# Attention scores one head at a time on quarter row tiles of TensorE, with all key and query rows resident

## What is computed

```
q = ((seq2 + b_self) @ Wq + bq)                # per head: 128 queries x 8
k = (concat[seq1 + b_prev, seq2 + b_self] @ Wk + bk)
score_prev = q @ k[:l1].T * SCALE              # masked with -inf where key >= seq_len1
score_self = (q * k[l1:]).sum(-1) * SCALE
weights    = softmax(concat[score_prev, score_self])
attn       = weights[:-1] @ v[:l1] + weights[-1:] * v[l1:]
x          = x + attn @ Wo + bo
```

## Time and profile before

| | |
|---|---|
| runs | 465.1, 459.02, 459.02 us; median 459.02 |
| profiled execution | 456.68 us, span 454.9 us, mean granted clock of TensorE 0.967 |
| PE busy | 427.5 us (94%), 2280 products |
| DVE, ACT, POOL busy | 336.1, 279.9, 185.5 us |
| DMA | 30.70 MB, mean 67 GB/s |

### The profile page before, as it was taken

How to read it: one execution, slowest core, us unless ns; L and a number is a source line. 1 busy time by engine, 2 the same in 40 slices (tenths; PEclk the granted TensorE clock), 3 DMA queues, 4 the chain that set the end, 5 groups by cost and what they waited for, 6 DMA issues and landing times.

```text
span 454.9 us, 7748 instructions
## 1 busy us (share of the span) xinstructions
PE 427.5 (94%) x2280; PEld 326.0 (72%) x2280; DVE 336.1 (74%) x598; ACT 279.9 (62%) x563; POOL 185.5 (41%) x235
## 2 busy tenths in 40 slices
PE   7799799799999999999999999999999988798985
PEld 3688678578788888878888887788888554454553
DVE  4897577696787779777777887776787776576763
ACT  5777476766555666655565766555655676476672
POOL 0868667572232233322242224226477424333330
PEclk9989899899999999999999999999999998888898
DMA  5525224200002020000201000010222624666430
GB/s 166 162 75 159 89 74 141 67 26 1 1 20 74 2 70 1 22 0 0 89 3 53 16 0 1 1 46 33 62 72 59 153 75 142 171 160 162 116 108 25
DMA packets 27908, 30.70 MB, mean 67 GB/s; under 512 B 4293, under 2 KB 22313, under 8 KB 27881
## 3 DMA queue, kind: packets, MB, share of 16 engines
q1 hardware_dynamic: 26680, 29.99, 22.8%
q0 software_dynamic: 768, 0.28, 0.4%
q10 hardware_dynamic: 432, 0.10, 0.1%
HBM read 22.73 MB, written 7.35 MB: 66 GB/s over the span
## 4 chain that ended last, share of the span: by engine, by line
PE 75%; DMA 10%; DVE 5%; issue 3%; ACT 3%; POOL 2%; SPq 1%; DVEq 0%; ACTq 0%; POOLq 0%
PE acc_ps L526 7%; PE u_ps L526 6%; PE acc_ps L528 6%; PE acc_ps L527 6%; PE g_ps L526 6%; PE g_ps L528 6%; PE g_ps L527 6%; PE u_ps L528 6%; PE u_ps L527 6%; DMA w_raw<-in_L_cond_Wu 4%; DMA k_plain<-k_rows 3%; PE pv_ps L702 3%; PE st_ps L692 2%; DMA q_blocks<-max_rows 2%; PE s_ps L594 2%
## 5 line engine op out<-in xcount | busy, mean ns | idle before, releaser
L841 ACT ACTIVATE act_p<-g_ps 128x512 f32<-128x512 f32 x144 | 85.9, 597 | 112.5 <-PE g_ps L528 112.0
L1135 DVE TENSOR_TENSOR act_p<-act_p,u_ps 128x512 f32<-128x512 f32 x144 | 98.6, 685 | 72.0 <-PE u_ps L528 40.5
L1139 DVE TENSOR_TENSOR act_lo<-act_p,act_hi 128x512 fp32r<-128x512 f32 x144 | 121.7, 845 | 0.4 <-ACT act_hi L846 0.4
L1380 POOL TENSOR_TENSOR xg_lo<-xg,xg_hi 128x512 fp32r<-128x512 f32 x35 | 50.1, 1432 | 149.9 <-ACT xg_hi L851 149.9
L846 ACT ACTIVATE act_hi<-act_p 128x512 fp32r<-128x512 f32 x144 | 89.9, 624 | 7.2 <-DVE act_p L1135 6.9
L526 PE MATMUL u_ps<-xg_hi,w_split 128*128 128x512 f32 x144 | 56.8, 395 | 7.4 <-issue 7.4
L526 PE MATMUL acc_ps<-act_hi,w_split 128*128 128x512 f32 x144 | 59.0, 410 | 0.0
L526 PE MATMUL g_ps<-x_hi,w_split 128*128 128x512 f32 (+1 forms) x144 | 57.5, 399 | 0.6 <-DVE x_lo L1168 0.6
L528 PE MATMUL acc_ps<-act_hi,w_split 128*128 128x512 f32 x144 | 56.9, 395 | 0.0
L527 PE MATMUL acc_ps<-act_lo,w_split 128*128 128x512 f32 x144 | 56.7, 394 | 0.0
L527 PE MATMUL g_ps<-x_lo,w_split 128*128 128x512 f32 (+1 forms) x144 | 56.7, 394 | 0.0
(11 more groups left out here) (193 smaller groups left out, 683.1 us busy)
## 6 DMA issues: line engine op xcount, KB each, us to landing
k_blocks<-k_rows SPq DMA_DIRECT2D x32, 96.0 KB
q_plain<-q_rows SPq DMA_DIRECT2D x8, 384.0 KB
q_blocks<-q_rows SPq DMA_DIRECT2D x32, 96.0 KB
k_plain<-k_rows SPq DMA_DIRECT2D x8, 384.0 KB
w_raw<-in_L_cond_Wg SPq DMA_DIRECT2D x8, 256.0 KB, 2.7
w_raw<-in_L_cond_Wu SPq DMA_DIRECT2D x8, 256.0 KB, 2.6
w_raw<-in_L_cond_Wd SPq DMA_DIRECT2D x8, 256.0 KB, 2.9
q_rows<-rows_hi SPq DMA_DIRECT2D x16, 128.0 KB
```

The lines of the kernel that those rows point to most:

```text
L841: activation(act_p[k % ACTS][:], g_ps[k % 3][:], ACT.Silu).then_inc(silu_done, 1)
L1135: tt(act_p[k % ACTS][:], act_p[k % ACTS][:], u_ps[k % 3][:], ALU.mult).then_inc(prod_done, 1)
L1139: tt(act_lo[k % ACTS][:], act_p[k % ACTS][:], act_hi[k % ACTS][:].bitcast(F32), ALU.subtract).then_inc(act_lo_done, 1)
L1380: tt(xg_lo[e % 3][:], xg[:].rearrange("p b s -> p (b s)"), xg_hi[e % 3][:].bitcast(F32), ALU.subtract)\
```

## The change

- `k_blocks`, `q_blocks`, `k_plain`, `q_plain` go. One tile, `key_query`, holds keys and queries of all eight pairs: group i's 24 rows lie on partitions 32i to 32i + 23, each head j in its own columns. Row 24 is the mask (keys) or ones (queries), rows 25 and 26 are ones (keys) or the two parts of the maxima (queries). The mask thus comes with the product, and ACT's bias and POOL's `pick_mask` go.
- A score is a product of one head: 25 rows (27 in the transposed kind) x 128 weights x 128 columns, four for a group. `both_scores` issues a group of either kind in turns; the s kind works on another group (`GROUPS`), so on other partitions and in another bank. Where only one kind stands, the four come one after another.
- PE's order in a pass is new: both scores of groups 0 and 1, `turn_max`, `turn_attn`, weigh two groups, both scores of group 2, weigh two groups, both scores of group 3, `project`, `turn_pv`. The loop of PE is written out.
- SP loads pairs 0 to 5 during the last tile, as POOL's fills of `key_query` end (768 KB and nine DMAs a pair), and pairs 6 and 7 in passes 4 and 5. `place_max` moves from POOL's queue to SP's: two DMAs a batch instead of one. ACT copies the max rows after the first exponential instead of before it.

```diff
-            def scores(b, n, i, bank=None):
+            def rows(m, p, g, count, j, n):
+                return key_query[ROW_TILE * g:ROW_TILE * g + count, p, m, j, half(n)]
...
+            def score(n, p, i, j, bank=None):
+                return mm((s_ps[i % 2] if bank is None else bank)[:, j * S:(j + 1) * S],
+                          rows(1, p, GROUPS[i], MAX_ROW, j, n), rows(0, p, GROUPS[i], MAX_ROW, j, n), start=True, stop=True)
...
+            def score_t(n, p, i, j):
+                return mm(st_ps[i % 2][:, j * S:(j + 1) * S], rows(0, p, i, MAX_ROW + 2, j, n), rows(1, p, i, MAX_ROW + 2, j, n),
+                          start=True, stop=True)
...
+            def both_scores(b, n, p, i, s_next):
+                if not s_next:
+                    return scores_t(b, n, p, i)
+                wait_scores(b + 2, n + 2, i)
+                wait_scores_t(b, n, i)
+                for j in range(GJ):
+                    last = score(n + 2, p + 1, i, j)
+                    last_t = score_t(n, p, i, j)
+                last.then_inc(s_written, 1)
+                last_t.then_inc(st_written, 1)
...
-            def body(b, n, s_next=True, turn_next=True):
-                if s_next:
-                    for i in range(2):
-                        scores(b + 2, n + 2, i)
+            def body(b, n, p, s_next=True, turn_next=True):
+                both_scores(b, n, p, 0, s_next)
+                both_scores(b, n, p, 1, s_next)
                 if turn_next:
                     turn_max(b + 1, n + 1)
-                for i in range(2):
-                    scores_t(b, n, i)
                 last_tile_step(b, 1)
...
                 if n >= 2:
                     turn_attn(b - 2, n - 2)
-                if s_next:
-                    scores(b + 2, n + 2, 2)
-                    scores(b + 2, n + 2, 3)
-                scores_t(b, n, 2)
+                weigh(b - 1, n - 1, 0)
+                weigh(b - 1, n - 1, 1)
+                both_scores(b, n, p, 2, s_next)
...
# SP
+            def load_pair(p):
+                for m, src in enumerate((k_rows, q_rows)):
+                    for i in range(GI):
+                        sp.dma_start(key_query[ROW_TILE * i:ROW_TILE * i + ONES_ROW, p, m] ... , src[p, ...]).then_inc(pair_loaded[p % 2], 16)
+                sp.dma_start(key_query[ONES_ROW:128:ROW_TILE, p, 0] ... , mask_row[...]).then_inc(pair_loaded[p % 2], 16)
+            def place_max(b):
+                sp.wait_ge(max_copied, b + 1)
+                for c in range(2):
+                    sp.dma_start(key_query[MAX_ROW + c:128:ROW_TILE, b // 2, 1, :, b % 2 * S:(b % 2 + 1) * S].bitcast(F32),
+                                 max_rows[b % 2][c * H:(c + 1) * H]).then_inc(max_placed[b % 2], 16)
...
+            for b in range(B):
+                place_max(b)
+                if b == 2:
                     later_stores(NT - 1)
+                if b in (4, 5):
...
+                    load_pair(p)
+                if b % 2 and b >= 5:
+                    store_out(b - 5, b - 3)
```

More of the change, by code:

```diff
@@ L198, in build @@
         SMALLS = 2 * (GI * GJ + GI * GJ + GI * GJ + 2 * H + S + H) + 4 * H * (DH + 1)
[L200 to L211, removed]
+        key_query = sb2("key_query", [128, NP, 2, GJ, PAIR * S], F32R)
+        FILLS = [(p, -(-(SMALLS + (p + 1) * 2 * GJ * PAIR * S) // (2 * 3 * F))) for p in range(NP)]
         probs_t = [sb2(f"probs_t{n}", [128, GJ, S]) for n in range(4)]
@@ L269, in build @@
         blocks_filled = sem("blocks_filled")
[L270 to L271 removed]
+        pair_loaded = [sem(f"pair_loaded{n}") for n in range(2)]
         max_placed = [sem(f"max_placed{n}") for n in range(2)]
@@ L683, in _, with wait_scores_t, scores_t @@
                     turn_max(EARLY_TURN[k], EARLY_TURN[k])
[L686 removed]
+            def wait_scores_t(b, n, i):
                 if i == 0:
[L689 removed]
                     pe.wait_ge(max_placed[n % 2], placed(b, n))
                 wait(pe, exp_done, b * GI + i - 1)
[L692 to L693 removed]
+            def score_t(n, p, i, j):
+                return mm(st_ps[i % 2][:, j * S:(j + 1) * S], rows(0, p, i, MAX_ROW + 2, j, n), rows(1, p, i, MAX_ROW + 2, j, n),
+                          start=True, stop=True)
+            def scores_t(b, n, p, i):
+                wait_scores_t(b, n, i)
+                for j in range(GJ):
+                    last = score_t(n, p, i, j)
+                last.then_inc(st_written, 1)
+            def both_scores(b, n, p, i, s_next):
+                if not s_next:
+                    return scores_t(b, n, p, i)
+                wait_scores(b + 2, n + 2, i)
+                wait_scores_t(b, n, i)
+                for j in range(GJ):
+                    last = score(n + 2, p + 1, i, j)
+                    last_t = score_t(n, p, i, j)
+                last.then_inc(s_written, 1)
+                last_t.then_inc(st_written, 1)
             def weigh(b, n, i):
@@ L1419, in _ @@
                 split_xg(NT - 1, e)
-                for tile, constant, experts in FILLS:
+                for p, experts in FILLS:
                     if e == min(experts + 2, NE - 1):
                         pool.wait_ge(down_done, SLOTS * (NT - 1) + experts * FC)
-                        nc.gpsimd.memset(tile[:].bitcast(F32), constant).then_inc(blocks_filled, 1)
-            def place_max(b, n):
-                pool.dma_start(q_blocks[n // 2 % 2][ROWS:ROWS + 2, :, :, n % 2 * S:(n % 2 + 1) * S]
-                               .rearrange("p j i s -> p (j i) s").bitcast(F32), max_rows[n % 2][:]).then_inc(max_placed[n % 2], 16)
+                        nc.gpsimd.memset(key_query[:, p].bitcast(F32), 1.0).then_inc(blocks_filled, 1)
             def split_max(b, n):
-                part = neg_max[n % 2][:].rearrange("p c (j i) -> p c i j", i=GI)
+                part = neg_max[n % 2][:].rearrange("p c (i j) -> p c i j", i=GI)
                 minus = minus_one[:].unsqueeze(2).to_broadcast([128, GI, GJ])
@@ L1463, in body @@
                     split_max(b + 2, n + 2)
-            for b in range(2):
-                pick_mask(b, b)
-                place_max(b, b)
             pool.wait_ge(down_done, SLOTS * NT)
```

147 lines of the change are left out of this document (47 added, 100 removed).

## The result

The changed kernel takes 497.16 us (median of 4 runs, 495.27 to 498.65), the kernel before 459.31 us on the same chip: a ratio of 1.082, 95% interval 1.075 to 1.089. It is **slower by 8%**, far above the forecast's 460 and outside its range. The profiled execution took 498.01 us, with a span of 496.1 us.

What follows compares the result with a forecast made beforehand. PE bounds the expert stage, DVE an undisturbed loop pass. Loop -6.2, early scores +4.7, first pass +2.5, SP +0.4, start -0.3 sum to +1.1 us on 456.68: 457.8 us profiled, 460 median, range 447 to 473.

Steps and rivals of the forecast that it cites:

- though nothing stalls: Attention loop: sign that the forecast is wrong, the granted clock falling without a stall; given no size and no chance.
- loads out of the loop: Attention loop: the reloads leave it, and with them 13.5 us of waits and slower clock over twelve passes.
- a pair of both kinds: Score groups: two products on different row groups run side by side at 0.112 us a pair, 0.45 us a group.
- a pass at full clock: Attention loop: PE's 2.76 us plus DVE's 2.31 us make 5.07 us; twelve passes 60.8 instead of 67.0 us, -6.2 us.
- an early block of four: Expert stage: eight lone score blocks cost 0.82 us each instead of 0.24, +4.7 us in all on PE.
- first block of eight, one kind: First pass, before the last down product: 1.27 us instead of 0.46, eight products in one group, two such blocks, +1.6 us.
- pairs 6 and 7: Loop, SP's queue: their loads delay later max rows by +0.4 us each at most, half taken, +0.4 us in the sum.
- weights in line: Rival, score pairs: weight loads don't run side by side, a pair costs 0.22 us, 474 us; chance 0.15.
- The max rows as the loop: Rival, attention loop: copy and DMA of the max rows set a pass of 5.93 us, 470 us; chance 0.12.
- DVE's pace: Rival, attention loop: a pass stays at 4.46 us, 453 us, or 449 with cheaper mode changes; chance 0.29.
- the lone blocks: Expert stage: if load and stream go in series, about 0.16 us a step, 1.3 us more for eight blocks; 0.112 preferred.
- A change between row tiles and the whole array and back: Around row-tiled blocks: 0.11 us on either side, then 0.11 us for weights no longer hidden.

Runs made afterwards that it cites:

- e15: e12 with the four spare products behind `turn_attn` moved into PE's wait ahead of `turn_pv` (none in the last two passes); 456.96 us, ratio 0.999 to the kernel before.
- e18: e15 with the spare products behind pass 3 on 25 rows instead of 128; 494.6 us, ratio 1.077 to the kernel before.
- e14: e2 with the entry of e9; 468.25 us, ratio 1.020 to the kernel before.
- e17: e1 with the entry of e9; 522.85 us, ratio 1.139 to the kernel before.
- e1: Changed kernel with both kinds of a group on the same 32 partitions, so no pair runs side by side; 530.27 us, ratio 1.165 to the kernel before.
- e5: e4 with PE's and ACT's order of the change, still two products of 512 columns per group; 449.64 us, ratio 0.983 to the kernel before.
- e13: e6 with the entry of e9; 470.72 us, ratio 1.026 to the kernel before.
- e2: Changed kernel with every score product on all 128 rows, exponentials scaled by 0; 524.24 us, ratio 1.151 to the kernel before.
- e6: Changed kernel with each group's four score products replaced by one of 25 (27) rows and 512 columns; 476.22 us, ratio 1.041 to the kernel before.
- e4: Kernel before without the loads of pairs 2 to 7, output wrong from batch 4 on; 445.8 us, ratio 0.979 to the kernel before.
- e16: e15 with `turn_attn` moved behind the four weighings; 457.38 us, ratio 1.000 to the kernel before.
- e3: Changed kernel with eight unread spare products of 128 rows and 256 columns in each pass; 521.37 us, ratio 1.145 to the kernel before.
- e7: Changed kernel with eight unread spare products of 128 rows and 384 columns in each pass with both kinds; two runs, 530.06 and 472.35 us.
- e9: Changed kernel with unread spare products (128 rows, 384 columns) only in the first body and passes 1 to 3; 485.9 us, ratio 1.064 to the kernel before.
- e11: Changed kernel with two groups of both kinds in turns on four row groups, plus e9's entry; 473.62 us, ratio 1.037 to the kernel before.
- e10: Changed kernel with e9's entry and the eight spare products of e7 in every pass with both kinds; 466.54 us, ratio 1.022 to the kernel before.
- e12: e11 with the eight spare products of 384 columns in all passes; 461.9 us, ratio 1.012 to the kernel before.

## Why the prediction was wrong

**The step that failed** is the one that was never priced: that the granted clock stays where it was if PE doesn't stall. The forecast named a fall of the clock "though nothing stalls" as what would make it wrong, gave it no chance and no time, and took every row at 2.4 GHz. The runs showed in its place a clock of 0.50 from 372.0 us to the end, with passes of 7.70 us in which PE never waits. Yet the earlier trace rows show that the kernel before loses the clock in this very part, and the change takes away the work on nearly all rows (97 and 98). The kernel before loses it three times in the loop, at 384.0, 394.2 and 418.1 us, each time for under 7 us, and gets it back; the changed kernel never does.

Two things were shown. First, **at full clock the rows decide whether it is kept**: e15 against e18 changes nothing but the rows of the spare products, and e14 against e17 says the same for the scores. In e17 and e18, as in e1, the clock fell without a wait of PE over 0.4 us ahead of it. Order and side-by-side issue are not it (e5, e1). For score products of 512 columns on few rows it isn't settled, as e13 lost the clock behind a wait. Second, **the level is sticky**: e2 and e14 do the same work in twelve passes, on all rows, one at 0.5 and one at 1.0, by the level at the entry. So half clock has two parts here, losing it and not getting it back. It did not come back to stay with all rows and 128 columns (e2) or with 512 columns and few rows (e6); it did come back where the scores had both (the kernel before, e4) and beside wide spare products on all rows in e16 and e17, though not in e3 nor, but for 3.4 us, in the traced execution of e7.

At the head of pass 1 of the changed kernel PE has waited 1.42 us (until 370.15), and the clock falls at 372.0. Few rows alone are not shown to be the cause of this first fall: e2, on all rows, lost the clock there too, at 375.6, behind a wait of 1.48 us; spare products on all rows in the waits (e9) prevented it, by their rows or because they fill the waits. What triggers a fall is not fully settled. In e9, e11 and e13 it came with a wait of 1.4 to 2.2 us, in e1, e17 and e18 without any, and the profiled execution of e5, on 97 and 98 rows, went through waits of up to 1.36 us unharmed.

The Trainium skill (TensorE: Matmul & The Clock Gate, What's actually happening) says that the gate sets the clock by how busy PE has been of late. By the busy time of the profile this doesn't hold here: e17 and e2 have PE busy for 36.00 of 36.00 us at 0.50, e14 for 35.98 of 36.00 at 1.00. That section says nothing of the rows of a product.

What each term did:

| term | forecast | measured |
|---|---|---|
| loads out of the loop | 13.5 us | 10.6 us (e4, medians) |
| a pair of both kinds | 0.112 us | 0.11 us; 0.21 at 1.2 GHz |
| a pass at full clock | 5.07 us | 4.94 us (e9, 4.85 without a spare product); in the changed kernel 7.70 at half clock |
| an early block of four | +0.58 us each | +0.56 each: eight slots grew by 4.46 us |
| first block of eight, one kind | 1.27 us | 0.80 us |
| pairs 6 and 7 | +0.4 us each | a wait of 1.4 us in e9; hidden at half clock |

The early blocks are seen on PE's timeline, `max_ps` in slot 22, to be read against the earlier trace rows:

```profile
326.85 0.39 PE L497 MATMUL acc_ps<-act_hi,w_split 128*128 128x512 f32 x1
327.17 0.66 PE L568 MATMUL max_ps<-key_query 25*128 25x128 f32 x4
327.75 0.50 PE L495 MATMUL g_ps<-x_hi,w_split 128*128 128x512 f32 x1
328.09 0.39 PE L496 MATMUL g_ps<-x_lo,w_split 128*128 128x512 f32 x1
```

From 326.85 to 328.09 there are 1.24 us, of which two products of 512 columns take 0.46: the block costs 0.78, where the forecast had 0.82. Between the first early product and the last `turn_max` there are 29.08 us (327.17 to 356.25), before 24.62. The block of eight in the first body:

```profile
360.93 0.39 PE L497 MATMUL acc_ps<-act_hi,w_split 128*128 128x512 f32 x1
361.25 0.67 PE L568 MATMUL s_ps<-key_query 25*128 25x128 f32 x8
361.85 0.50 PE L495 MATMUL acc_ps<-act_hi,w_split 128*128 128x512 f32 x1
362.19 0.39 PE L496 MATMUL acc_ps<-act_lo,w_split 128*128 128x512 f32 x1
```

By the same measure this block costs 1.26 - 0.46 = 0.80 us, where the forecast had 1.27. From its start to the next product eight take 0.60 us and four 0.58: group 1 starts beside group 0, though its products stand behind in the program. The forecast had all eight in one group and in line, but the code puts them on two row groups.

**What the clock cost.** Twelve passes of 7.70 instead of 4.94 us are 33.1 us. The last three steps from one `turned_ps` to the next took 6.85, 6.75 and 3.00 us; in e15, at full clock, 4.11, 3.59 and 1.90: 7.0 us more. 498.0 - 33.1 - 7.0 = 457.9 us, an estimate beside the forecast's 457.8 for the profiled execution. That close is partly luck: a block of eight was forecast too dear and the wait of 1.4 us too cheap, and the estimate leaves out what the 8.8 us at half clock ahead of the twelve passes cost (372.0 to 380.82), and the waits for pairs 6 and 7 that passes at full clock would show. So the sum of the mechanisms came within some us, with its verdict of no gain, and nearly all of the miss of 40 us is the clock. e15 bears this out: with the clock kept, two groups at once and spare products it takes 456.96 us.

The rivals: weights in line is refuted (0.11 us a pair, though e1 prices it: 10.32 - 7.70 = 2.6 us a pass at half clock). The max rows as the loop: not seen; SP's `place_max` ends no pass but the one behind pair 6. DVE's pace: not reached, 4.94 against 4.46. For the lone blocks the forecast worked out 0.16 us a step, load and stream in series, from the rule that weight loads overlap running products only where the row group differs (the Trainium skill, TensorE: Matmul & The Clock Gate, The mechanism). The steps took 0.11 us, in the early blocks and on all rows in e14 (420.05, 420.16), so 0.16 was wrong. The rule as it stands there doesn't fit either: products of 512 columns on nearly all or all rows, each with weights of its own, start 0.23 to 0.24 us apart, and the load for the product of 334.07 starts at 333.84, beside the product of 333.83. Whether the 0.11 us are a load alone or a shorter load and the stream is open.

## What to carry to other kernels

Before cutting a product into row tiles, ask what clock it will run at: a saving of zeros in the array (here three quarters of the rows) can come with the loss of half the clock. Price such a loop at both levels, 1.2 and 2.4 GHz, and give the lower one a chance, above all where PE waits a microsecond or two at the loop's entry. If the clock is lost, look for idle time of PE in which a product on all rows costs nothing (with products that nobody reads e10 is 31 us faster than the changed kernel, and e15, which has two groups at once besides, 40 us), and check that the loop is entered at full clock.

## What the runs showed that was not expected

- The granted clock of a loop with PE busy throughout can be 0.50 for 120 us. Entered at full clock, it was kept on 128 rows (e14) and lost on 25 and 27 (e17).
- The same loop stays at either level, by how it is entered: 524.24 us (e2) and 468.25 (e14). One kernel, e7, took 530.06 and 472.35 us.
- Four row groups run at a time: sixteen products of 128 columns in four steps of 0.11 us (e12). Groups on different rows run side by side even if they stand one after the other in the program (0.60 us for eight products, 0.58 for four).
- A change between row tiles and the whole array and back costs 0.34 us (a block takes 0.78 us, its four steps 0.44). This was expected from one product in the earlier trace rows, and holds.
